# A graph-attention edge stage on one Trainium2 core: node ranges of 128 that start at multiples of 64, and gathers held to three groups ahead

## The chip, the cores and the metric

The kernel runs on one core of a Trainium2 chip. The metric is the device time of one execution in microseconds (us); the median of three runs of the kernel before is 867.32 us (866.72 to 867.4). Engines: PE is the matrix engine (TensorE), DVE is VectorE, ACT is ScalarE, POOL is GpSimd, SP is SyncE.

## The reference, cut to what matters

A graph attention layer over 2,500 nodes and 40,000 edges sorted by destination, then a mixture-of-experts layer. Only the first is touched:

```python
h = layernorm(x) @ W + b_w
s_dst, s_src = h @ a[:512], h @ a[512:]
e = leaky_relu(s_dst[dst] + s_src[src] + b_a, negative_slope=0.2)
w = jnp.exp(e)
alpha = w / segment_sum(w, dst)[dst]
x1 = x + segment_sum(alpha[:, None] * h[src], dst)
# then x1 + sum over the top 2 of 8 experts of share * (gelu(layernorm(x1) @ W1 + b1) @ W2 + b2)
```

## The kernel before, in words

**Three stages.** The node stage computes h for 20 tiles of 128 nodes and stores a table of rows of 516 floats in DRAM: h in two halves of 256, a one behind the first half (its sum is the denominator), and the two scores of the source. The edge stage sums weighted rows into `acc`, one slice of 2 x 257 floats for each tile of 128 nodes. The expert stage follows, once `acc` is divided and added to x.

**Edge stage.** The 40,000 edges are 313 chunks of 128, in 79 groups of four chunks (`GC`; the last group has one chunk). An average group of 512 sorted edges reaches over 2,500 / 79, some 32 nodes. Five engines work on a group g:

- POOL (`gather`, L501 to L509) issues one indirect DMA for each chunk, four a group, into slot g % 8 of the ring `rows` (`RING` is 8). It waits for the counter `agg_ok`, that is, until PE has done the sums of group g - 7. Its code is written out for all 79 groups.
- ACT (`weights`, L945) waits until all four chunks of the group are there (`got`), and for DVE's maximum of group g - 1 (the one PSUM buffer `ps_E2` is used again). It makes exp(s_dst + s_src) and exp(0.2 (s_dst + s_src)) for every edge of a chunk and all 128 nodes of the group's tile: eight instructions of 128 x 128.
- DVE (`step_of_group`, L1275) waits for ACT, computes the edge's lane in the tile (`lanes`, L1220), the larger of the two weights (`largest`, L1215), and four masks (`masked`, L1225), which keep a weight only where the node is the edge's own. Behind the masks of group g it adds the sums of group g - 2 to `acc` (`add_group`, L1290, and `add`, L1233), after a wait for `agg_ok`.
- PE (`group` and `sums`, L709 and L701) waits for the masks of group g and for `added` of group g - 2 (two pairs of PSUM banks take turns), and multiplies: 4 chunks x 2 halves of 257 columns, each float32 product two records in the trace, so 16 records a group. Its last one counts up `agg_ok`.

**Tiles that a group leaves.** A group whose edges go over from one tile of 128 nodes to the next has an extra round (`extras`, L1262, L955, and the loop at L718): ACT makes eight more activations for the next tile, DVE adds the sums of the extra before, makes lane, maximum and masks again, and PE does 16 more records into a third pair of banks (`ps_agg[2]`). One extra is added at the very end (L1321). A table of words, made on DVE at L1198 to L1212, tells every engine a group's tile, its number of extras, and how many came before.

**Order of the work.** Each engine runs its own program in order. ACT and PE loop over eight groups, DVE over four. POOL starts once the table of nodes is in DRAM (L512 to L514). ACT starts its first group when `sdst_b`, the destination scores of all nodes on all partitions, is copied from PSUM (L940 to L943) and the words are there.

Of the kernel before, what the change touches and what calls it, by code (L numbers as in the profile page):

```python
# [20 lines left out]
def gnn_moe_kernel(nc, x, src, dst, gnn_W, gnn_b_w, gnn_a, gnn_b_a, Wg, bg, W1, b1, W2, b2, out):  # L21
# [9 lines left out]
    RING = 8  # L31
    U = 4
# [8 lines left out]
    ONE, S_SRC = HD, 2 * HALF - 1  # L41

# [15 lines left out]
    with ExitStack() as ctx:  # L58
# [38 lines left out]
        acc = sg("acc", [P, NT, 2, HALF], F32, first)  # L97
# [143 lines left out]
        ps_E2, ps_id = ps[6].rearrange("p (c n) -> p c n", c=GC), ps[7][:, 0:P]  # L241
# [34 lines left out]
        acc_ok, added, xadded = sem("acc_ok"), sem("added"), sem("xadded")  # L276
# [84 lines left out]
        def tile_in(word):  # L361
            return field(word, 0, 31, NT - 1)

        def extra_in(word):
            return field(word, 5, 31, NT - 1)

        def before_in(word):
            return field(word, 10, 4095, NG * NT)

        def tile_of(value):  # L370
            return nc.s_assert_within(value, 0, NT - 1, skip_runtime_bounds_check_because="a tile of the window")
# [116 lines left out]
        def _(pool):  # L488
# [9 lines left out]
            nc.gpsimd.iota(node_id[:, :], pattern=[[1, NTN]], base=0, channel_multiplier=0)  # L498
# [376 lines left out]
        def _(act):  # L875
# [69 lines left out]
            def weights(q, r, tile, n=GC):  # L945

                low = E2x[:, 0, :, :] if q == 2 else ps_E2
                for k, (e, scale) in enumerate(((E1[:, q, :, :], 1.0), (low, SLOPE))):
                    for c in range(n):
                        bias = rows[:, r, c, S_SRC + k:S_SRC + k + 1]  # L950
                        m = nc.scalar.activation(e[:, c, :], sdst_b[:, bass.ds(tile * P, P)], ACT.Exp,  # L951
                                                 bias=bias, scale=scale)
                return m

            def extras(r, chunks):  # L955
# [3 lines left out]
                with act.If(extra > 0):  # L959
                    tile, before = act.snap(tile_in(word)), act.snap(before_in(word))  # L960
                    with act.Fori(0, extra) as n:
                        act.wait_ge(xmax_ok, before + n + 1)
                        weights(2, r, tile_of(tile + n + 1), chunks).then_inc(xexp_ok, 1)

            def group(r, i, chunks=GC):
                tile = act.snap(tile_in(act.snap(regs[r])))
                act.wait_ge(max_ok[(r + 1) % 2], RING // 2 * i + (r + 1) // 2 + 1)
                act.wait_ge(got[r], 16 * GC * (i + 1) if chunks == GC else 16 * (GC * i + chunks))
                weights(r % 2, r, tile, chunks).then_inc(exp_ok, 1)
                extras(r, chunks)  # L970

            act.wait_ge(d_ok, len(ps_d))
# [118 lines left out]
        def _(dve):  # L1091
# [116 lines left out]
            nc.vector.scalar_tensor_tensor(out=win_w[:, 0, BACK:NG + BACK], in0=win_n[:, 0, :], scalar=32.0,  # L1208
                                           in1=win_i[:, 0, :], op0=ALU.mult, op1=ALU.add)
            link(nc.vector.tensor_copy(win_w[:, 1, BACK + 1:NG + BACK], win_n[:, 1, 0:NG - 1]))  # L1210
            nc.vector.scalar_tensor_tensor(out=window[:, :], in0=win_w[:, 1, :], scalar=1024.0, in1=win_w[:, 0, :],
# [8 lines left out]
            def lanes(w, g, tile):  # L1220

                return nc.vector.tensor_tensor(lane[:, w, :], dstT[:, bass.ds(GC * g, GC)],  # L1222
                                               node_id[:, bass.ds(tile * P, 1)].to_broadcast([P, GC]), ALU.subtract)
# [9 lines left out]
            def add(q, tile, count):  # L1233
                a = acc[:, bass.ds(tile, 1), :, :].rearrange("p t a d -> p (t a) d")
# [325 lines left out]
```

## Time and profile before

| | |
|---|---|
| median of 3 runs | 867.32 us |
| the profiled execution: span from first to last instruction | 861.7 us |
| PE busy in the span | 696.6 us (81%) |
| DVE, ACT, POOL busy | 457.2, 415.4, 457.3 us |
| mean granted clock of PE | 0.921 |
| first gather of the edge stage issued | 92.24 us |
| last gather issued | 549.00 us |
| last addition to `acc` starts | 573.35 us |

The profile gives the span; of the time around it, it shows nothing, and the median lies 5.6 us above the span. Busy time counts matmuls as they are issued; their ends are modelled. A releaser "issue" means that the engine waited for nothing that the profile shows, "remote" that it was released by a semaphore whose sender is not told. In the rows below, `mean ns of one` is the duration of one instruction, and times of a timeline are counted from the start of the span.

### The profile page before, as it was taken

The page shows a single profiled execution, that of the slowest core. Times are in us where ns is not written, and L with a number is a line of the kernel's source. Part 1 is how long each engine was busy: PE and PEld are TensorE (multiplying, and loading weights), DVE is VectorE, ACT ScalarE, POOL GpSimd, SP SyncE. Part 2 cuts the span into 40 slices and gives each one's busy share as a digit, 9 for nine tenths or more (in the row PEclk, how much of TensorE's full clock was granted, in tenths as well). Part 3 has the DMA queues.
Part 4 walks back from the last instruction along what each step waited for, and adds up shares of the span by engine and source line. Part 5 has one row for each costly group of instructions (what it writes and reads, how often), then busy time and mean ns, then how long its engine had stood idle before and what let it go on. Part 6 is the DMA issues. An engine that isn't in the chain of part 4 may idle for free.

```text
span 861.7 us, 14833 instructions
## 1 busy us (share of the span) xinstructions
PE 696.6 (81%) x3260; PEld 553.6 (64%) x3261; DVE 457.2 (53%) x1232; ACT 415.4 (48%) x1134; POOL 457.3 (53%) x530
## 2 busy tenths in 40 slices
PE   4999355879888787879788888959889999999960
PEld 3777245657766666667676767845547787888840
DVE  5998223555555555556465555668485433333320
ACT  4443442545545554536455545618754444545430
POOL 5000575666666666666666666310105677777750
PEclk9999687998989899989999898988988999999995
DMA  5342576666666666666656666407993577777768
GB/s 197 117 155 92 156 213 164 172 188 168 186 181 174 178 177 182 186 171 183 189 166 184 176 179 179 118 27 283 334 380 127 104 131 131 135 131 135 130 91 250
DMA packets 58299, 146.96 MB, mean 171 GB/s; under 512 B 8868, under 2 KB 18708, under 8 KB 57880
## 3 DMA queue, kind: packets, MB, share of 16 engines
q0 software_dynamic: 35216, 106.84, 50.6%
q1 hardware_dynamic: 22968, 37.16, 12.3%
q10 hardware_dynamic: 80, 2.56, 1.0%
q8 instruction: 14, 0.23, 0.1%
q14 instruction: 21, 0.17, 0.1%
HBM read 118.17 MB, written 33.47 MB: 176 GB/s over the span
## 4 chain that ended last, share of the span: by engine, by line
PE 40%; issue 19%; DVE 11%; DMA 11%; ACT 4%; POOL 4%; POOLq 2%; DVEq 2%; another core or an unknown queue 2%; ACTq 1%; SPq 1%
PE ps L705 30%; DMA result<-y,si 8%; PE ps L659 3%; POOL rows L506 2%; DMA x_all<-in_x_dram 2%; ACT E L951 2%; ACT ps L951 2%; PE ps L844 1%; DVE Wt L1217 1%; PE ps L785 1%; DVE S L1228 1%; DVE acc L1235 1%; PE ps L755 1%; POOL xg L593 1%
## 5 line engine op out<-in xcount | busy, mean ns | idle before, releaser
L705 PE MATMUL ps<-rows,S 128*128 128x257 f32 x1556 | 383.4, 404 | 98.7 <-issue 83.9
L506 POOL DMA_INDIRECT rows<-node_table,srcT x313 | 301.8, 964 | 234.4 <-issue 83.8
L705 PEld LDWEIGHTS ps<-rows,S 128*128 128x128 f32 x1556 | 312.3, 202 | 169.6 <-issue 121.3
L951 ACT ACTIVATE E<-sdst_b,rows 128x128 f32 x389 | 124.0, 389 | 236.2 <-DVE Wt L1217 120.7
L1235 DVE TENSOR_TENSOR acc<-acc,ps 128x514 f32 x99 | 68.0, 687 | 116.1 <-remote 77.6
L1228 DVE SCALAR_TENSOR_TENSOR S<-ps,lane,Wt 128x128 f32<-128x128 f32 x389 | 109.6, 345 | 4.4 <-issue 0.8
L951 ACT ACTIVATE ps<-sdst_b,rows 128x128 f32 x313 | 96.2, 351 | 2.0 <-issue 2.0
L844 PE MATMUL ps<-W_e,xgT 128*128 x352 | 83.4, 380 | 0.0
L602 POOL DMA_INDIRECT result<-y,si x44 | 70.4, 1601 | 11.4 <-issue 7.1
L1222 DVE TENSOR_TENSOR lane<-dstT,node_id 128x4 f32 (+1 forms) x98 | 16.1, 164 | 111.5 <-issue 77.0
L844 PEld LDWEIGHTS ps<-W_e,xgT 128*128 128x128 f32 x352 | 63.4, 190 | 6.9
L659 PE MATMUL ps<-Wb,xT 128*128 128x512 f32 x240 | 59.1, 403 | 2.5 <-DVE dstT L1184 1.4
L858 PE MATMUL ps<-W_hi,hidT 128*128 x176 | 55.6, 437 | 3.0 <-DVE hidT L1512 2.8
L1058 ACT ACTIVATE act_h<-hid 128x256 f32<-128x256 f32 x44 | 18.4, 418 | 77.2 <-DVE hid L1519 67.2
L1529 DVE TENSOR_TENSOR y_b<-ps,b_b 128x512 f32<-128x512 f32 x44 | 30.4, 692 | 46.4 <-PE ps L858 39.4
L659 PEld LDWEIGHTS ps<-Wb,xT 128*128 128x128 f32 x240 | 45.6, 194 | 12.6 <-DVE dstT L1184 1.6
L1217 DVE SCALAR_TENSOR_TENSOR Wt<-E,ps 128x512 f32<-128x512 f32 (+1 forms) x79 | 53.3, 675 | 0.0
L593 POOL DMA_INDIRECT xg<-xn_table,gi x44 | 48.1, 1094 | 8.1 <-issue 4.6
L1519 DVE TENSOR_TENSOR hid<-ps,b_b 128x256 f32<-128x256 f32 x44 | 18.7, 424 | 55.1 <-PE ps L844 51.3
L551 POOL COPY si<-dst_row 128x1 int32 (+1 forms) x45 | 31.9, 709 | 19.0 <-DVE need L1503 11.9
L858 PEld LDWEIGHTS ps<-W_hi,hidT 128*128 128x128 f32 x176 | 32.6, 188 | 11.8 <-issue 5.9
L548 POOL COPY gi<-src_row 128x1 int32 (+1 forms) x45 | 9.7, 215 | 54.0 <-DVE src_row L1458 35.9
(203 smaller groups left out, 678.8 us busy)
## 6 DMA issues: line engine op xcount, KB each, us to landing
W_e<-in_L_ffn_W_dram SPq DMA_DIRECT2D x16, 512.0 KB, 8.5
node_table<-rows SPq DMA_DIRECT2D x20, 258.0 KB, 2.7
result<-acc SPq DMA_DIRECT2D x20, 256.0 KB, 2.5
xn_table<-xn SPq DMA_DIRECT2D x20, 256.0 KB, 2.2
rows<-node_table,srcT POOLq DMA_INDIRECT x313
x_all<-in_x_dram SPq DMA_DIRECT2D x19, 256.0 KB, 3.1
out_dram<-result SPq DMA_DIRECT2D x1, 2500.0 KB, 16.7
out_dram<-result ACTq DMA_DIRECT2D x1, 2500.0 KB, 18.4
```

The lines of the kernel that those rows point to most:

```text
L506: nc.gpsimd.indirect_dma_start(out=rows[:, g % RING, c, :], out_offset=None, in_=table, in_offset=bass.IndirectOffsetOnAxis(ap=srcT[:, GC ...
L551: nc.gpsimd.tensor_copy(si[:, r, :], dst_row[:, bass.ds(i, 1)]).then_inc(si_ok, 1)
L593: nc.gpsimd.indirect_dma_start(out=xg[:, r, :], out_offset=None, in_=xn_table, in_offset=bass.IndirectOffsetOnAxis(ap=gi[:, r, :], axis=0) ...
L602: nc.gpsimd.indirect_dma_start(out=result, out_offset=bass.IndirectOffsetOnAxis(ap=si[:, (r - LAG) % YR, :], axis=0), in_=y[:, (r - LAG) % ...
L659: m = pe.matmul(ps_h[s][j][:, :], xT[:, s, a, k, j * P:(j + 1) * P], Wb[:, b, k, :], start=(n == 0), stop=(n == 3 * KT - 1))
L705: m = pe.matmul(ps_agg[q][:, a, 0:HALF], S[:, w, c, :], rows[:, r, c, a * HALF:(a + 1) * HALF], start=(c == 0), stop=(c == n - 1))
L844: m = pe.matmul(ps_hid[1 - s][:, 0:F], xgT[:, 1 - s, k * P:(k + 1) * P], W1_e[:, bass.ds(e, 1), k, :].rearrange("p e f -> p (e f)"), start ...
L858: m = pe.matmul(ps_y[s][:, :], hidT[:, s, a, k * P:(k + 1) * P], W[:, bass.ds(e, 1), k, :].rearrange("p e d -> p (e d)"), start=(c == 0), ...
L951: m = nc.scalar.activation(e[:, c, :], sdst_b[:, bass.ds(tile * P, P)], ACT.Exp, bias=bias, scale=scale)
L1217: return nc.vector.scalar_tensor_tensor(out=Wt[:, q, 0:n, :], in0=E1[:, q, 0:n, :], scalar=FINITE, in1=(E2x[:, 0, 0:n, :] if q == 2 else p ...
L1228: m = nc.vector.scalar_tensor_tensor(out=S[:, w, c, :], in0=ps_id[:, :], scalar=lane[:, w, c:c + 1], in1=Wt[:, q, c, :], op0=ALU.is_equal, ...
L1235: nc.vector.tensor_tensor(a, a, ps_agg[q][:, :, 0:HALF], ALU.add).then_inc(count, 1)
```

## The change

Ranges of nodes ("windows") are still 128 wide, but start at multiples of 64, so there are 40 of them (`NW`); an even one is a tile, an odd one is the upper half of one tile and the lower half of the next. A group takes the window that starts at or below its first node, and has an extra only if it reaches 64 nodes or more beyond that window's half. The destination scores `sdst_w` are kept once for each window: ACT copies the even ones from PSUM as before, two new DVE copies make the odd ones. Partition p of an odd window stands for node 64 + p modulo 128 of its pair of tiles, so that `acc` need not move: the masks compare with numbers from `ps_id` that are turned by 64 for an odd window, and `add` is two instructions of 64 partitions, each into its own tile. The gather of group g waits for the sums of group g - 3 in place of g - 7; the ring keeps its eight slots. The code for extras stays.

```diff
+    AHEAD = 3
+    HP = P // 2
+    NW = 2 * NT
...
-        acc = sg("acc", [P, NT, 2, HALF], F32, first)
+        acc = sg("acc", [P, NT + 1, 2, HALF], F32, first)
...
-        sdst_b = sg("sdst_b", [P, NTN], F32, first)
+        sdst_w = sg("sdst_w", [P, NW, P], F32, first)
-        node_id = sg("node_id", [P, NTN], I16, first)
+        ring_id = sg("ring_id", [P, 3 * HP], I16, first)
+        base = sg("base", [P, NW], I16, first)
...
             def gather(g):
 
-                if g >= RING - 1:
-                    pool.wait_ge(agg_ok, g - RING + 2)
+                if g >= AHEAD:
+                    pool.wait_ge(agg_ok, g - AHEAD + 1)
...
-                nc.scalar.activation(sdst_b[:, 4 * b * P:4 * b * P + n], ps_d[b][:, 0:n], ACT.Copy).then_inc(d_ok, 1)
+                nc.scalar.activation(sdst_w[:, 8 * b:8 * b + 2 * n // P:2, :],
+                                     ps_d[b][:, 0:n].rearrange("p (t n) -> p t n", n=P), ACT.Copy).then_inc(d_ok, 1)
...
-            act.wait_ge(d_ok, len(ps_d))
+            act.wait_ge(odd_ok, 2)
...
-            link(nc.vector.tensor_single_scalar(win_i[:, :, :], win_i[:, :, :], 7, ALU.arith_shift_right))
-            link(nc.vector.tensor_tensor(win_n[:, 0, :], win_i[:, 1, :], win_i[:, 0, :], ALU.subtract))
+            link(nc.vector.tensor_single_scalar(win_i[:, :, :], win_i[:, :, :], HP.bit_length() - 1, ALU.arith_shift_right))
+            link(nc.vector.tensor_single_scalar(win_i[:, 0, :], win_i[:, 0, :], NW - 2, ALU.min))
+            link(nc.vector.tensor_tensor(win_i[:, 1, :], win_i[:, 1, :], win_i[:, 0, :], ALU.subtract))
+            link(nc.vector.tensor_single_scalar(win_i[:, 1, :], win_i[:, 1, :], 1, ALU.arith_shift_right))
+            link(nc.vector.tensor_copy(win_n[:, 0, :], win_i[:, 1, :]))
...
-            def masked(q, w, n=GC):
-
+            def masked(q, k, w, n=GC):
+
+                turn_of = dve.snap((w & 1) * HP)
                 for c in range(n):
                     m = nc.vector.scalar_tensor_tensor(
-                        out=S[:, w, c, :], in0=ps_id[:, :], scalar=lane[:, w, c:c + 1],
+                        out=S[:, k, c, :], in0=ps_id[:, bass.ds(turn_of, P)], scalar=lane[:, k, c:c + 1],
                         in1=Wt[:, q, c, :], op0=ALU.is_equal, op1=ALU.mult)
                 return m
 
-            def add(q, tile, count):
-                a = acc[:, bass.ds(tile, 1), :, :].rearrange("p t a d -> p (t a) d")
-                nc.vector.tensor_tensor(a, a, ps_agg[q][:, :, 0:HALF], ALU.add).then_inc(count, 1)
+            def add(q, w, count):
+
+                for part, tile in ((slice(HP, P), w >> 1), (slice(0, HP), (w + 1) >> 1)):
+                    a = acc[part, bass.ds(tile, 1), :, :].rearrange("p t a d -> p (t a) d")
+                    m = nc.vector.tensor_tensor(a, a, ps_agg[q][part, :, 0:HALF], ALU.add)
+                m.then_inc(count, 1)
...
             dve.wait_ge(d_ok, len(ps_d))
+            dve.wait_ge(ids_ok, 1)
+            nc.vector.tensor_copy(sdst_w[:, 1:NW:2, HP:P], sdst_w[:, 0:NW:2, HP:P]).then_inc(odd_ok, 1)
+            nc.vector.tensor_copy(sdst_w[:, 1:NW - 1:2, 0:HP], sdst_w[:, 2:NW:2, 0:HP]).then_inc(odd_ok, 1)
...
-            den = acc[:, :, 0, ONE]
+            den = acc[:, 0:NT, 0, ONE]
```

Left out of the diff: the fields of the words become one bit wider, names change from `tile` to `w`, extras step by two windows, and POOL fills `ring_id`, `base` and a corner of `sdst_w` in the node stage.

## Rows read from the trace of the kernel before

**Rows 1.** Busy time by stretch: start:end and length, then each engine's busy us (count), clock, DMA share, GB/s

```profile
92.00:166.00 74.00, 40.88 (x155) 33.34 (x156) 24.95 (x72) 26.89 (x90) 49.53 (x52) 0.77 0.67 186
308.00:355.00 47.00, 38.28 (x163) 31.16 (x162) 25.70 (x73) 25.69 (x86) 31.05 (x32) 0.96 0.65 177
544.00:575.00 31.00, 26.53 (x122) 22.51 (x120) 19.87 (x57) 12.56 (x42) 4.72 (x5) 1.00 0.17 48
```

**Rows 2.** Costliest groups of the page: busy us, mean ns of one, idle before

```profile
L705 PE MATMUL ps<-rows,S 128*128 128x257 f32 x1556 | 383.4, 404 | 98.7 <-issue 83.9
L506 POOL DMA_INDIRECT rows<-node_table,srcT x313 | 301.8, 964 | 234.4 <-issue 83.8
...
L1235 DVE TENSOR_TENSOR acc<-acc,ps 128x514 f32 x99 | 68.0, 687 | 116.1 <-remote 77.6
```

**Rows 3.** Timeline, first groups: start, duration, engine, line, count, idle before

```profile
92.24 1.15 POOL L506 DMA_INDIRECT rows<-node_table,srcT  x1 [78.54 <-DMA node_table<-rows]
...
96.22 0.95 POOL L506 DMA_INDIRECT rows<-node_table,srcT  x1 [0.30 <-issue]
...
100.09 1.28 ACT L951 ACTIVATE E<-sdst_b,rows 128x128 f32 x4 [8.20 <-DMA rows<-node_table,srcT]
101.21 0.95 POOL L506 DMA_INDIRECT rows<-node_table,srcT  x1 [0.30 <-issue]
...
102.73 0.16 DVE L1222 TENSOR_TENSOR lane<-dstT,node_id 128x4 f32<-128x4 f32 x1 [11.48 <-ACT ps L951]
...
103.53 1.13 DVE L1228 SCALAR_TENSOR_TENSOR S<-ps,lane,Wt 128x128 f32<-128x128 f32 x4
...
104.71 8.80 PE L705 MATMUL ps<-rows,S 128*128 128x257 f32 x32 [15.06 <-issue]
...
105.15 1.28 ACT L951 ACTIVATE E<-sdst_b,rows 128x128 f32 x4 [2.65 <-DMA rows<-node_table,srcT]
```

**Rows 4.** Timeline, who was released by the first two groups' sums

```profile
119.33 0.69 DVE L1235 TENSOR_TENSOR acc<-acc,ps 128x514 f32 x1 [4.64 <-remote]
...
137.08 0.95 POOL L506 DMA_INDIRECT rows<-node_table,srcT  x1 [4.91 <-remote]
```

**Rows 5.** Timeline of POOL: two gathers that waited, one group apart

```profile
195.88 0.94 POOL L506 DMA_INDIRECT rows<-node_table,srcT  x1 [2.41 <-remote]
201.89 0.94 POOL L506 DMA_INDIRECT rows<-node_table,srcT  x1 [1.32 <-PE ps L705]
```

**Rows 6.** Timeline, a stretch in which PE and DVE step slowly

```profile
288.39 0.38 PE L705 MATMUL ps<-rows,S 128*128 128x257 f32 x1 [2.43 <-issue]
...
289.82 0.16 DVE L1222 TENSOR_TENSOR lane<-dstT,node_id 128x4 f32 x1 [6.88 <-issue]
```

**Rows 7.** Timeline, the release of one group's sums late in the stage

```profile
319.96 0.94 POOL L506 DMA_INDIRECT rows<-node_table,srcT  x1 [2.19 <-remote]
319.97 0.69 DVE L1235 TENSOR_TENSOR acc<-acc,ps 128x514 f32 x1 [4.41 <-remote]
320.81 4.37 PE L705 MATMUL ps<-rows,S 128*128 128x257 f32 x19 [0.76 <-DVE acc L1235]
```

**Rows 8.** Timeline, the end of the edge stage

```profile
546.31 25.43 PE L705 MATMUL ps<-rows,S 128*128 128x257 f32 x116 [1.20 <-issue]
...
549.00 0.95 POOL L506 DMA_INDIRECT rows<-node_table,srcT  x1 [0.30 <-issue]
...
572.06 0.69 DVE L1235 TENSOR_TENSOR acc<-acc,ps 128x514 f32 x1 [0.21 <-DVE acc L1235]
573.35 0.69 DVE L1235 TENSOR_TENSOR acc<-acc,ps 128x514 f32 x1 [0.60 <-DVE acc L1235]
```

**Rows 9.** Busy time by stretch, columns as in the first group: the clock in the first groups

```profile
108.10:118.10 10.00, 5.41 (x25) 4.31 (x24) 3.44 (x11) 5.16 (x18) 7.56 (x9) 1.00 0.76 212
...
125.10:128.30 3.20, 1.17 (x6) 0.68 (x4) 0.00 (x0) 1.82 (x6) 2.59 (x3) 1.00 0.76 210
128.50:142.00 13.50, 4.07 (x10) 3.27 (x11) 3.60 (x11) 0.74 (x2) 6.77 (x7) 0.50 0.50 138
```

More of the change, by code:

```diff
@@ L358, in field, with window_in, window_of @@
                                       skip_runtime_bounds_check_because="the table's words are built so")
-        def tile_in(word):
-            return field(word, 0, 31, NT - 1)
+        def window_in(word):
+            return field(word, 0, 63, NW - 1)
         def extra_in(word):
-            return field(word, 5, 31, NT - 1)
+            return field(word, 6, 31, NT - 1)
         def before_in(word):
-            return field(word, 10, 4095, NG * NT)
-        def tile_of(value):
-            return nc.s_assert_within(value, 0, NT - 1, skip_runtime_bounds_check_because="a tile of the window")
+            return field(word, 11, 4095, NG * NT)
+        def window_of(value):
+            return nc.s_assert_within(value, 0, NW - 1, skip_runtime_bounds_check_because="a window of the nodes")
         block = ctx.enter_context(nc.Block())
@@ L942, in _, with weights @@
                 n = min(4, NT - 4 * b) * P
-                nc.scalar.activation(sdst_b[:, 4 * b * P:4 * b * P + n], ps_d[b][:, 0:n], ACT.Copy).then_inc(d_ok, 1)
-            def weights(q, r, tile, n=GC):
+                nc.scalar.activation(sdst_w[:, 8 * b:8 * b + 2 * n // P:2, :],
+                                     ps_d[b][:, 0:n].rearrange("p (t n) -> p t n", n=P), ACT.Copy).then_inc(d_ok, 1)
+            def weights(q, r, w, n=GC):
                 low = E2x[:, 0, :, :] if q == 2 else ps_E2
@@ L950, in weights @@
                         bias = rows[:, r, c, S_SRC + k:S_SRC + k + 1]
-                        m = nc.scalar.activation(e[:, c, :], sdst_b[:, bass.ds(tile * P, P)], ACT.Exp,
+                        m = nc.scalar.activation(e[:, c, :], sdst_w[:, bass.ds(w, 1), :].rearrange("p w n -> p (w n)"), ACT.Exp,
                                                  bias=bias, scale=scale)
@@ L1240, in settle, with weigh_extra, add_extra @@
                 nc.vector.memset(spare[:, 0:1], 0.0)
-            def weigh_extra(g, tile, at, chunks):
+            def weigh_extra(g, w, at, chunks):
                 dve.wait_ge(xS_ok, at)
                 dve.wait_ge(xexp_ok, at)
-                lanes(SR, g, tile)
+                lanes(SR, g, w)
                 largest(2, chunks).then_inc(xmax_ok, 1)
                 dve.wait_ge(xmax_ok, at + 1)
-                masked(2, SR, chunks).then_inc(xS_ok, 1)
-            def add_extra(n_added, tile, at):
+                masked(2, SR, w, chunks).then_inc(xS_ok, 1)
+            def add_extra(n_added, w, at):
                 if n_added is not None:
@@ L1254, in add_extra @@
                 dve.wait_ge(xagg_ok, at + 1)
-                add(2, tile, xadded)
+                add(2, w, xadded)
                 settle(xadded, at + 1)
-            last_tile = dve.alloc_register("last_extra_tile")
-            dve.reg_mov(last_tile, 0)
+            last_window = dve.alloc_register("last_extra_window")
+            dve.reg_mov(last_window, 0)
             def extras(g, n_added, word, chunks):
@@ L1265, in extras @@
                 with dve.If(extra > 0):
-                    tile, before = dve.snap(tile_in(word)), dve.snap(before_in(word))
-                    add_extra(n_added, tile_of(dve.snap(last_tile)), before)
-                    weigh_extra(g, tile_of(tile + 1), before + 1, chunks)
+                    w, before = dve.snap(window_in(word)), dve.snap(before_in(word))
+                    add_extra(n_added, window_of(dve.snap(last_window)), before)
+                    weigh_extra(g, window_of(w + 2), before + 1, chunks)
                     with dve.If(extra > 1):
                         with dve.Fori(1, extra) as n:
-                            add_extra(n_added, tile_of(tile + n), before + n)
-                            weigh_extra(g, tile_of(tile + n + 1), before + n + 1, chunks)
-                    dve.reg_mov(last_tile, tile + extra)
+                            add_extra(n_added, window_of(w + n + n), before + n)
+                            weigh_extra(g, window_of(w + n + n + 2), before + n + 1, chunks)
+                    dve.reg_mov(last_window, w + extra + extra)
             def step_of_group(g, r, i, first=False, chunks=GC):
@@ L1280, in step_of_group @@
                     dve.wait_ge(S_ok, g - 1)
-                tile = dve.snap(tile_in(word))
-                lanes(r % SR, g, tile)
+                w = dve.snap(window_in(word))
+                lanes(r % SR, g, w)
                 largest(r % 2, chunks).then_inc(max_ok[r % 2], 1)
                 dve.wait_ge(max_ok[r % 2], U // 2 * i + r // 2 + 2)
-                masked(r % 2, r % SR, chunks).then_inc(S_ok, 1)
+                masked(r % 2, r % SR, w, chunks).then_inc(S_ok, 1)
                 if not (first and r < 2):
@@ L1303, in _ @@
             dve.wait_ge(ids_ok, 1)
-            nc.vector.tensor_copy(ps_id[:, :], node_id[:, 0:P]).then_inc(id_ok, 1)
+            nc.vector.tensor_copy(ps_id[:, :], ring_id[:, :]).then_inc(id_ok, 1)
             dve.wait_ge(id_ok, 1)
```

33 lines of the change are left out of this document (18 added, 15 removed).

## The prediction

> **What bounds the kernel now.** I read the table of stretches first, then the costliest groups, then timelines of single groups.
>
> The edge stage runs from the first gather at 92.24 us to the last addition, which ends at 573.35 + 0.69 = 574.04 us: 482 of 861.7 us of span. The change touches nothing behind it. A stretch of eight groups takes about 47 us, and no engine fills it: PE 38.3, POOL 31.1, DVE and ACT 25.7 us [rows 1]. PE does 1,556 records: 79 groups are 78 x 16 + 4 = 1,252, and 19 extras of 16 are the other 304 [rows 2]. DVE's 99 additions tell the same: 79 + 19 + one at the end. PE's rate undisturbed is 25.43 / 116 = 0.219 us a record [rows 8], 3.5 us for 16.
>
> POOL is busy 0.96 us for a gather but starts one only every 1.25 us: 101.21 - 96.22 = 4.99 us for four [rows 3]. So 313 gathers need at least 391 us, 5.0 us a group. They take 549.00 - 92.24 = 456.8 us, 5.86 us a group. The difference is waiting for `agg_ok`. Then 25 us pass from the last gather to the last addition, with PE busy nearly throughout [rows 1, 8]: PE lies up to seven groups behind.
>
> **Two oddities matter.** First, what follows PE's sums is released late. PE issued groups 0 and 1 by 104.71 + 8.80 = 113.5 us [rows 3]; the addition of group 0 starts at 119.33, and the gather that needs group 1, that of group 8, at 137.08 [rows 4]. Again at 319.96 and 319.97 POOL and DVE are released together, after POOL had issued nothing for over 2 us [rows 7]. Where POOL issues just one group between two waits, the step is 201.89 - 195.88 = 6.01 us [rows 5], of which 4.7 are issues. Second, while gathers stream, PE and DVE sometimes crawl: gaps of 2.4 us before one matmul and 6.9 us before one lane instruction, with nothing to wait for [rows 6].
>
> **The change part by part.** The sum is made against the profiled execution, whose span stands 5.6 us below the median of 867.32; I carry the difference in time over to the median.
>
> Extras. A group of 512 edges reaches over some 32 nodes, a window from a multiple of 64 leaves at least 64, so I expect none. PE loses 304 records, 304 x 0.219 = 67 us, and DVE loses 19 additions, lanes, maxima and masks, ACT 19 x 8 activations. It is no term of the sum: whatever bounds the stage next takes its place. It would be POOL, at 5.0 us a group, if gathers could run ahead.
>
> The gather's wait. It closes a loop over three groups: gathers of g, their landing, ACT, DVE, PE, gathers of g + 3. Step by step:
> - four issues, first start to last end: 3 x 1.25 + 0.95 = 4.70 us [rows 3];
> - landing and ACT's start: 100.09 - (96.22 + 0.95) = 2.92, and 105.15 - (101.21 + 0.95) = 2.99: I take 2.95 [rows 3];
> - ACT's eight activations and the step to DVE: 102.73 - 100.09 = 2.64 [rows 3];
> - lane, maximum, masks: 103.53 + 1.13 - 102.73 = 1.93 [rows 3];
> - the additions of group g - 2, for which PE's sums of group g wait, stand behind these masks. One takes 0.687 us [rows 2]. Two halves of 64 partitions: between 0.69 us (if half the partitions took half the time) and 2 x 0.69. No row shows an instruction on 64 partitions. I take the upper end, since its 514 elements in a partition are as before; less the 0.1 us by which an addition starts before the masks end: 1.27;
> - DVE's addition to PE: 320.81 - (319.97 + 0.69) = 0.15 [rows 7];
> - 16 records of sums: 3.50 [rows 8];
> - release: 572.06 - (546.31 + 25.43) = 0.32, the nearest undisturbed one [rows 8].
>
> Together 17.46 us for three groups, 5.82 a group. That is over POOL's 5.0, so POOL waits every time. PE needs 3.5, DVE about 0.16 + 0.68 + 1.1 + 1.4 = 3.3 and ACT 2.5 us of it, so none becomes the bound, and the second addition costs time only as a link of the loop. The register steps for the turned numbers and for the second tile go beside running instructions, except some 0.1 us that may stand before the masks; as the bound I take three of the shortest DVE instructions seen, 3 x 0.16 us [rows 3], up to 0.5 us a loop, or 13 us in all.
>
> End of the stage. Group 78 follows group 0 by 26 loops: its gather starts at 92.24 + 26 x 17.46 = 546.2 us. It has one chunk, so group 77 is later: gathers from 102.46 (group 2's start, one step after 97.47) + 25 x 17.46 = 539.0, sums issued until 539.0 + 17.14 = 556.1, plus 0.9 for group 78: 557.0. Then the additions of groups 77 and 78 and of the last extra: before, they end 574.04 - 571.74 = 2.3 us behind PE; three more instructions of 0.69 make 4.4. End: 561.4, or 12.6 us earlier. The gain is the vanished backlog of PE, not the pace of the gathers, which hardly changes (5.82 against 5.86).
>
> Preparation. The two DVE copies of the odd windows (1,280 and 1,216 elements a partition) and three short steps for the words stand before ACT's first group. By 514 elements in 0.69 us [rows 2] they take 1.7 us each. ACT waits 8.2 us and DVE 11.5 us for the first rows at that time [rows 3], which hides them. If that cover were gone it would cost 4 us. A POOL that could not issue beside them would lose up to 3.4 us; I take 0.6. The Trainium skill ("SBUF — State Buffer", on the "DVE blocks DMA" trap) says that such a copy locks GpSimd out of descriptor writing while it runs. By it the first gather moves by up to the length of both copies; no row here shows such a pair.
>
> Sum: -12.6 + 0.6 = -12.0, that is 855 us.
>
> **The rivals.**
>
> *The release stays late, no change.* If PE's signal only gets through when the stream of gathers pauses, POOL's step is 6.01 us as in [rows 5], not 5.82. Then group 78 starts at 102.5 + 76 x 6.01 = 559.2; the end lies about 15.2 us behind (as 561.4 - 546.2), 574.4: 867 to 868 us. For it: [rows 4, 7]. Against: those signals came while PE had a backlog, here it has none.
>
> *PE falls to the low clock, slower.* PE will work 3.5 of 5.8 us and rest 2.3. In the first groups it was like that: the clock stayed at 1.00 (2.4 GHz) with PE busy 5.4 of 10 us, but went to 0.50 (1.2 GHz) after a stretch with 1.17 of 3.2 us [rows 9]. At 1.2 GHz sums take 3.5 us more, and the loop 21.0. It decides the sign once one loop in seven is hit: 26 x 3.5 / 7 = 13 us. One in three gives 855 + 26 x 3.5 / 3 = 885 us, every one 946. For it: the falls in [rows 9] follow scarce work. Against: 0.77 in the first stretch came with much longer rests. The Trainium skill ("TensorE: Matmul & The Clock Gate", "The HAM clock gate") calls the throttled state the default, which activity releases. By that rule a less busy PE loses clock, and the time is that of this rival.
>
> *POOL is the bound.* If the loop closes within 15 us, it is 5.0 us a group: 92.2 + 391 + 15 = 498, 76 us less, 791 us. It needs 2.5 us less than the rows give, such as landing in a quieter DMA (2.95 us is all of that link) or additions out of the way. Half of it (halves of additions at half time, landing 1 us shorter) gives a loop of 15.8: 43 us less than the forecast, 812 us.
>
> *The change doesn't do what it says*, and extras remain: then more than the loop's 17.46 us, by about 3.5 us an extra. A group of 64 nodes or more would be needed.
>
> **How the numbers follow.** 855 with chance 0.42; late release (862 to 872) 0.2; low clock (over 869) 0.28; a shorter loop (under 840) 0.09; extras 0.01. The range takes in both ends of the additions (26 x 0.69 = 18 us less) and of the register steps (13 us more), and low clock up to one loop in three: 835 to 885. The likeliest case's own range is 845 to 863. A measurement of this kernel can tell 0.2%, 1.7 us, from no change. Faster: 0.42 + 0.09 and 0.03 of the late release, 0.54; within 0.2%: 0.1; slower: 0.36.
>
> **What would show it.** 1,252 records of L705 and no E2x activations; 313 gathers, of which every fourth waits about 0.8 us, and steps of 5.8 us; 160 additions (two for each group and for the last extra) of 0.69 us; the last addition some 15 us behind the last gather; crawls as in [rows 6] gone. A step of 5.0 would show that I mis-sized the loop, 6.0 the late release, a clock below 0.9 in the stage the second rival.

## The result, and the profile after

The changed kernel takes 920.84 us (median of four runs, 911.06 to 933.7) where the kernel before takes 867.36 (866.72 to 867.48): a ratio of 1.057, interval 1.054 to 1.060. The slowest of the four, 933.7, lies over 1.5% above the fastest and is left out of the ratio. The forecast was 855 with a range of 835 to 885, so sign and range were both wrong. The profiled execution has a span of 909.4 us (861.7 before) and a mean granted clock of 0.882 (0.921 before).

The costliest groups of the page, columns as in [rows 2]:

```profile
L712 PE MATMUL ps<-rows,S 128*128 128x257 f32 x1252 | 348.8, 443 | 178.8 <-DVE acc L1249 149.2
L513 POOL DMA_INDIRECT rows<-node_table,srcT x313 | 296.2, 946 | 300.0 <-PE ps L712 111.3
...
L1249 DVE TENSOR_TENSOR acc<-acc,ps 64x514 f32 x160 | 110.1, 688 | 6.3 <-PE ps L712 1.9
```

There are 1,252 records and 160 additions, so no extras are left. The 304 fewer records, 67 us at the undisturbed rate, lower PE's busy time by only 383.4 - 348.8 = 34.6 us: the remaining ones are slower, 443 ns in place of 404. An addition of 64 partitions takes 0.688 us, the same as one of 128.

Busy time by stretch, columns as in [rows 1]:

```profile
92.00:166.00 74.00, 42.87 (x144) 34.08 (x144) 32.35 (x84) 26.55 (x86) 41.98 (x44) 0.77 0.57 160
...
214.00:261.00 47.00, 32.91 (x123) 26.42 (x122) 23.11 (x58) 17.96 (x60) 25.29 (x27) 0.83 0.54 149
261.00:308.00 47.00, 31.38 (x108) 24.82 (x107) 22.59 (x55) 15.61 (x52) 27.54 (x31) 0.82 0.59 165
308.00:355.00 47.00, 32.09 (x122) 25.23 (x121) 24.84 (x63) 18.11 (x61) 26.52 (x29) 0.89 0.56 159
...
575.00:626.00 51.00, 32.22 (x121) 25.55 (x119) 27.52 (x66) 15.12 (x50) 20.85 (x32) 0.86 0.39 110
```

PE has 32 of 47 us to do and runs at a clock of 0.82 to 0.89; before it had 38 us and 0.96. Some 29 gathers fall into 47 us where there were 32.

The timeline at the start and at the end of the edge stage:

```profile
93.15 0.83 DVE L1317 COPY sdst_w<-sdst_w 128x1280 f32<-128x1280 f32 x1
...
93.89 0.82 DVE L1318 COPY sdst_w<-sdst_w 128x1216 f32<-128x1216 f32 x1
94.33 1.34 POOL L513 DMA_INDIRECT rows<-node_table,srcT  x1 [81.89 <-DMA node_table<-rows]
...
102.36 1.28 ACT L959 ACTIVATE E<-sdst_w,rows 128x128 f32 x4 [7.42 <-DMA rows<-node_table,srcT]
...
607.72 0.94 POOL L513 DMA_INDIRECT rows<-node_table,srcT  x1 [2.00 <-PE ps L712]
...
622.64 1.39 DVE L1249 TENSOR_TENSOR acc<-acc,ps 64x514 f32 x2 [0.65 <-DVE acc L1249]
```

The stage runs from 94.33 to 622.64 + 1.39 = 624.03 us. It ends 50 us later than before (574.04), and 909.4 - 624.0 = 285.4 us lie behind it (287.7 before). So the loss is all in this stage. Its last gather starts 26 loops after its first: (607.72 - 94.33) / 26 = 19.75 us a loop of three groups, where the prediction has 17.46.

One such loop, from the first gather of a group to the first gather of the third group after it. The other groups' rows are left out:

```profile
258.82 0.94 POOL L513 DMA_INDIRECT rows<-node_table,srcT  x1 [3.89 <-PE ps L712]
...
262.57 0.95 POOL L513 DMA_INDIRECT rows<-node_table,srcT  x1 [0.30 <-issue]
...
264.33 3.74 PE L712 MATMUL ps<-rows,S 128*128 128x257 f32 x16 [2.31 <-DVE acc L1249]
...
266.54 1.28 ACT L959 ACTIVATE E<-sdst_w,rows 128x128 f32 x4 [6.21 <-DMA rows<-node_table,srcT]
...
269.26 0.16 DVE L1233 TENSOR_TENSOR lane<-dstT,base 128x4 f32 x1 [4.99 <-ACT ps L959]
269.34 0.68 DVE L1228 SCALAR_TENSOR_TENSOR Wt<-E,ps 128x512 f32<-128x512 f32 x1
270.25 1.12 DVE L1240 SCALAR_TENSOR_TENSOR S<-ps,lane,Wt 128x128 f32<-128x128 f32 x4 [0.23 <-issue]
...
271.41 1.39 DVE L1249 TENSOR_TENSOR acc<-acc,ps 64x514 f32 x2
...
272.95 9.51 PE L712 MATMUL ps<-rows,S 128*128 128x257 f32 x32 [4.88 <-DVE acc L1249]
...
279.26 0.94 POOL L513 DMA_INDIRECT rows<-node_table,srcT  x1 [4.08 <-PE ps L712]
```

The whole is 279.26 - 258.82 = 20.44 us. Link by link: issues until 263.52, 4.70; landing until 266.54, 3.02; ACT until 269.26, 2.72; lane, maximum and masks until 271.37, 2.11; additions until 272.80, 1.43; PE starts 0.15 later; then 6.31 us until POOL goes on. That last link is the odd one: 3.50 + 0.32 was forecast. The clock during it, columns as above:

```profile
264.20:268.20 4.00, 3.74 (x16) 2.95 (x16) 0.07 (x1) 1.66 (x6) 3.09 (x4) 1.00 0.77 215
268.20:272.90 4.70, 0.00 (x0) 0.00 (x0) 3.26 (x8) 1.96 (x8) 2.19 (x3) 0.78 0.51 140
272.90:278.70 5.80, 5.75 (x16) 4.72 (x17) 3.27 (x8) 1.67 (x7) 1.89 (x2) 0.59 0.54 155
278.70:282.50 3.80, 3.76 (x18) 2.94 (x16) 1.32 (x5) 1.94 (x7) 2.58 (x3) 1.00 0.33 83
```

PE works at 1.00 (2.4 GHz), rests for 4.9 us, and while it rests the mean clock falls to 0.78. The 16 records after the rest take 5.75 us at 0.59, that is some four fifths of this time at the lower level (0.5, 1.2 GHz). The next 18 are at 1.00 again. This recurs: of the 78 full sets of sums, 32 take over 4.2 us from their first to their last start, 5.0 us in the median where undisturbed ones take 3.3, and in most of the stage it is every third set. All 14 sets that began over 4 us after the start of PE's record before were slow, and none of the 32 that began within 2 us; of the 31 between, 17 were.

### The profile page after: what moved, and what is told of

Its sections match the earlier page's. It is cut to its first block, busy times and chain, and to the rows that moved or that the text cites. A ratio compares the mean times of both kernels' runs of the same rounds, so it can differ in the third digit from the quotient of the medians.

```text
span 909.4 us, 13772 instructions
## 1 busy us (share of the span) xinstructions
PE 660.4 (73%) x2956; PEld 517.4 (57%) x2957; DVE 467.9 (51%) x1165; ACT 370.4 (41%) x982; POOL 450.5 (50%) x533
## 4 chain that ended last, share of the span: by engine, by line
PE 31%; issue 18%; POOL 13%; DVE 13%; DMA 10%; ACT 5%; DVEq 3%; another core or an unknown queue 2%; POOLq 1%; ACTq 0%; SPq 0%
POOL rows L513 12%; PE ps L712 11%; DMA rows<-node_table,srcT 6%; PE ps L851 5%; PE ps L865 4%; PE ps L666 3%; ACT ps L959 2%; DVE acc L1249 2%; DMA result<-y,si 2%; PE ps L762 2%; ACT E L959 2%; DVE Wt L1228 2%; PE ps L841 1%; DVE S L1240 1%
## 5 line engine op out<-in xcount | busy, mean ns | idle before, releaser
L712 PE MATMUL ps<-rows,S 128*128 128x257 f32 x1252 | 348.8, 443 | 178.8 <-DVE acc L1249 149.2
L513 POOL DMA_INDIRECT rows<-node_table,srcT x313 | 296.2, 946 | 300.0 <-PE ps L712 111.3
L712 PEld LDWEIGHTS ps<-rows,S 128*128 128x128 f32 x1252 | 276.7, 226 | 250.7 <-issue 184.0
L959 ACT ACTIVATE E<-sdst_w,rows 128x128 f32 x313 | 100.0, 390 | 329.3 <-DMA rows<-node_table,srcT 322.1
L1233 DVE TENSOR_TENSOR lane<-dstT,base 128x4 f32 (+1 forms) x79 | 13.2, 167 | 245.4 <-ACT ps L959 158.0
L1249 DVE TENSOR_TENSOR acc<-acc,ps 64x514 f32 x160 | 110.1, 688 | 6.3 <-PE ps L712 1.9
L1240 DVE SCALAR_TENSOR_TENSOR S<-ps,lane,Wt 128x128 f32<-128x128 f32 x313 | 88.2, 345 | 18.7 <-issue 11.1
L959 ACT ACTIVATE ps<-sdst_w,rows 128x128 f32 x313 | 95.9, 350 | 0.0
## 6 DMA issues: line engine op xcount, KB each, us to landing
out_dram<-result ACTq DMA_DIRECT2D x1, 2500.0 KB, 18.1
```

The costliest lines, as they stand in the source:

```text
L513: nc.gpsimd.indirect_dma_start(out=rows[:, g % RING, c, :], out_offset=None, in_=table, in_offset=bass.IndirectOffsetOnAxis(ap=srcT[:, GC ...
L712: m = pe.matmul(ps_agg[q][:, a, 0:HALF], S[:, w, c, :], rows[:, r, c, a * HALF:(a + 1) * HALF], start=(c == 0), stop=(c == n - 1))
L959: m = nc.scalar.activation(e[:, c, :], sdst_w[:, bass.ds(w, 1), :].rearrange("p w n -> p (w n)"), ACT.Exp, bias=bias, scale=scale)
L1240: m = nc.vector.scalar_tensor_tensor(out=S[:, k, c, :], in0=ps_id[:, bass.ds(turn_of, P)], scalar=lane[:, k, c:c + 1], in1=Wt[:, q, c, :], ...
L1249: m = nc.vector.tensor_tensor(a, a, ps_agg[q][part, :, 0:HALF], ALU.add)
```

## The experiments

Each ratio is against the kernel before in the same job, on the same chip. The chips differ: the kernel before took 787.9 us (786.1 to 789.9) in the first job and 868.8, 869.9 and 863.8 in the three others. The first job's chip is called the fast chip here.

**Fill TensorE's rest.** Ten products of the identity with itself go into an unused corner of PSUM after each set of sums, for groups 0 to 71:

```diff
                 sums(r % 2, r % SR, r, chunks).then_inc(agg_ok, 1)
+                if not (isinstance(g, int) and g >= RING):
+                    for _ in range(10):
+                        pe.matmul(ps[5][:, 384:512], ident[:, :], ident[:, :], start=True, stop=True)
```

> The changed kernel, with ten float32 products of 128 x 128 that nobody reads behind the sums of each of groups 0 to 71, in a bank of PSUM that the sums do not use. They fill PE's rest (about 0.107 us a record, 20 records, 2.1 us) and are nothing to the result. Clock theory (the loop of three groups costs 17.9 us at 2.4 GHz, and one set of sums at 1.2 GHz on the same chain of groups adds some 2.3 us each time round): the clock in the edge stage goes to 0.98 or more, no set of sums takes over 3.6 us from first to last issue, the loop falls from 20.2 to about 18 us, and the time to 867 to 878 us. Rival (the late release of PE's signal while gathers stream is what costs, and more records on PE make it later): clock up, but steps between gathers stay at 6.6 us and the time stays over 905 us.

Measured on the fast chip: 876.76 us (873.78 to 880.74), ratio 1.115, interval 1.111 to 1.119; first to last gather 479.9 us, 18.46 us a loop. Time and loop are as expected; two of the 78 full sets are still slow.

> The changed kernel (gathers three ahead) with ten small products a group that fill PE's rest, as in the first run with warm filling, on whichever chip this job gets (the kernel before took 788 us on one and 869 us on another). Theory A: the loop of three groups is latency bound and its half-clock set of sums is the larger part of the loss; then this kernel does not depend on the chip, 870 to 882 us, with every set of sums at 3.3 us, and on a chip where the kernel before takes 868 it is 1 to 2% slower than it, so five sixths of the changed kernel's loss is clock. Theory B: late release of the gathers adds to it on the chips where before shows it: over 890 us there, with late waits in the trace. Theory C: the products themselves cost more than they save on such a chip: as slow as the changed kernel, 911 to 930.

> The changed kernel itself, unchanged, beside the other runs of this job. Theory A: its loop of three groups is latency and clock bound, with no term that differs between chips, so it is 911 to 930 us on any chip, also where before takes 788 (a ratio of 1.17 there, 1.06 to 1.07 on the others). Theory B: late release makes part of its loss on the slower chips: then on a chip where before takes 788 it is 10 to 30 us shorter, 885 to 905 us, with no late wait.

On a slower chip the filled kernel takes 878.68 us (876.29 to 883.51), ratio 1.0095, interval 1.007 to 1.012, and the changed kernel beside it 914.08 us (905.4 to 921.17), ratio 1.054, interval 1.048 to 1.060 (1.06 to 1.07 was expected). One stretch of the two, the filled one first:

```profile
261.00:308.00 47.00, 44.17 (x278) 40.13 (x277) 24.73 (x60) 18.26 (x61) 28.96 (x31) 1.00 0.61 169
```

```profile
261.00:308.00 47.00, 32.51 (x122) 25.51 (x120) 23.79 (x60) 16.87 (x56) 26.74 (x29) 0.87 0.57 158
```

More work for PE, 12 us in 47, makes the kernel 914.1 - 878.7 = 35.4 us faster: only 3 sets of sums are slow in place of 31. The filled kernel takes the same on both chips within 2 us, though the kernel before differs by 82 us between them. So of the changed kernel's loss of 914.1 - 869.9 = 44 us, 35 us or four fifths went with the slow sets (five sixths were expected). The late releases of the gathers went too: 18 in the changed kernel's profile of this job, 28 us in sum, against 24 short ones, 12 us. What each was worth is worked out behind the experiments. That the changed kernel itself does not depend on the chip is not shown, for it did not come onto the fast one.

**Each half of the change alone.** The windows without the wait (lead back at seven groups), and the wait without the windows:

```diff
-    AHEAD = 3
+    AHEAD = 7
```

> The changed kernel with AHEAD = 7, so that a gather waits for the sums of the group seven back, as before. Loop theory (the wait of three groups is what made it slower): the loop then allows 17.9 / 7 = 2.6 us a group, POOL's 5.0 us or the release of PE's signals bounds; between 795 us (POOL alone, 5.0 us a group) and 860 us. Rival (windows of 64, with two additions a group and the turned masks, cost what was lost): no faster than 900 us.

```diff
-                if g >= RING - 1:
-                    pool.wait_ge(agg_ok, g - RING + 2)
+                if g >= 3:
+                    pool.wait_ge(agg_ok, g - 2)
```

> The kernel before with one line changed: the gather waits for the sums of the group three back. Loop theory: the loop is one addition and the register steps shorter (16.9 us at the high clock), but every fourth group has an extra of 16 records and a second round on ACT and DVE in it (about 4 us more each), so 6.3 us or more a group, 900 to 950 us. Rival (the windows are the cause): within 2% of 867 us.

On the fast chip the windows alone take 790.28 us (788.03 to 794.34), ratio 1.004, interval 1.002 to 1.005, 5 us under the range that was expected; the wait alone 885.15 us (884.09 to 889.51), ratio 1.125, interval 1.122 to 1.129. A stretch of the windows alone, and then the stage's gathers in that kernel:

```profile
261.00:308.00 47.00, 35.38 (x153) 27.93 (x152) 31.05 (x78) 21.94 (x73) 35.43 (x39) 1.00 0.75 212
```

```profile
L513 POOL DMA_INDIRECT rows<-node_table,srcT x313 | 296.4, 947 | 177.3 <-issue 95.1 <-DMA node_table<-rows 82.2
```

POOL waits for nothing in the stage but its own issuing: 38 gathers in 47 us, 5.0 us a group (485.16 - 94.64 = 390.5 us for all). That is the rival "POOL is the bound", whose 791 us came true for the lead of seven, on this chip. There the wait is what costs, with or without the windows. The wait alone came out below the 900 us and more that was expected: with its extras PE is busy 36 of 47 us and rests less, and the clock is 0.90 where the changed kernel, on another chip, has 0.82 to 0.89. That this is the reason is not tested:

```profile
261.00:308.00 47.00, 36.26 (x145) 29.52 (x145) 22.07 (x64) 21.61 (x72) 28.47 (x31) 0.90 0.64 178
```

**One addition for two.** All 128 partitions are added to one tile, so the halves of odd windows go to the wrong nodes:

```diff
-                for part, tile in ((slice(HP, P), w >> 1), (slice(0, HP), (w + 1) >> 1)):
+                for part, tile in ((slice(0, P), w >> 1),):
```

> The changed kernel with one addition of 128 partitions a group, into the lower tile alone (sums of odd windows go to wrong rows for half the nodes, which no wait depends on). Loop theory: the second addition is a link of the loop; 0.69 us less for three groups, 26 x 0.7 = 18 us less than the changed kernel's 911 to 934 us, if the clock falls as often. Rival (additions lie beside other work): no more than 3 us less.

One run took 901.5 us; first to last gather is 512.1 us, 19.70 us a loop, no better than the 19.69 to 20.16 of the changed kernel's three profiles. In 253 cases the next record of a set starts 0.40 to 0.50 us later, the pace of the low clock (256 in the profile above). Taking 0.69 us out of a link gave no visible gain in the loop, against the 18 us expected, and the trace shows where it went: from a group's first gather to its sums the way is 13.30 us in place of 14.06, but the 26 sets on the chain that sets the pace are all slow and take 6.0 us in the median, where the changed kernel's slow sets take 5.0. They begin 6.4 us after the start of PE's record before, in the median (3.8 in the changed kernel). No gather was released late in this run, so the slow sets alone make a loop of 19.70 us. On the run's total nothing is concluded: it is a single run on another chip.

**The lead between three and seven, on slower chips.** Beside them a profile of the kernel before and one of the changed kernel:

> The kernel before, unchanged, for its profile on the chip of the experiments. Late-release theory (what held the kernel before at 867 us was PE's signals coming through only when the gathers paused, and that differs from chip to chip): where the kernel before takes 788 us, its profile shows no wait of POOL for agg_ok, gathers every 5.0 us a group, and no stretch in which PE and DVE step every 0.7 us; where it takes 867 us, the waits and the slow stretches are there again. Rival (the matmuls or the DMA themselves are faster there): records closer than 0.217 us, or landings well under 2.9 us.

> The changed kernel, unchanged, beside the others of this job. Loop theory: it waits in every group, for a loop that holds no signal held back by the stream if the chip has none; so 900 to 925 us on any chip, and against a kernel before of 788 us a ratio of 1.14 to 1.17. Rival (the chip matters as much as for the kernel before): 80 us less than 920, about 840 us.

> The changed kernel with AHEAD = 7 once more. On a chip where the kernel before takes 788 us: 788 to 794 us again. On a chip where it takes 867 us: the release theory says that POOL now streams with six groups of room, so PE's signals wait for a pause that comes late: 820 to 880 us, with stretches of slow steps on PE and DVE longer than before; POOL-bound theory says 800 us or less there too.

> The changed kernel with AHEAD = 5. Loop theory: 17.9 us over five groups is 3.6 us a group, and even 20.3 us is 4.1, both under POOL's 5.0: no wait is left where no signal is late, and the time is that of AHEAD = 7 within 3 us. Rival (any wait nearer than the ring costs): between AHEAD 7 and 3, 20 us or more over AHEAD 7.

> The changed kernel with the lead of the gathers four groups in place of three. Theory A: a lead of three loses because its loop (18.0 us undisturbed, 20.3 with a half-clock set) must pass for every three groups. With four groups in the loop it gives 20.3/4 = 5.1 us a group, so the loop is no longer what holds the gathers; on this chip, where a stream of gathers without a pause lets TensorE's signals through late, the late releases come back and the time is that of a lead of five, 852 to 866 us. Theory B: the half-clock sets come with any wait for the sums and lengthen the loop further: a lead of four lies between, 875 to 900 us. Where before takes 788, theory A gives 786 to 800.

| lead | us (range) | ratio, interval | starts at the low clock's pace | us a group |
|---|---|---|---|---|
| before, 7 | 868.82 (867.32 to 871.84) | 1 | 125 of 1,556 records | 5.93 |
| 3 | 926.72 (911.04 to 930.02) | not used | 245 of 1,252 records | 6.72 |
| 4 | 851.76 (851.14 to 854.55) | 0.9875, 0.985 to 0.991 | 168 | 5.83 |
| 5 | 858.08 (857.75 to 859.42) | 0.988, 0.985 to 0.990 | 161 | 5.88 |
| 7 | 864.23 (863.31 to 866.07) | 0.995, 0.993 to 0.997 | 167 | 5.88 |

A start counts where the next record starts 0.40 to 0.50 us later, within a set; the pace is first to last gather by 78. The lead of four was in a later job, where the kernel before took 863.83. The changed kernel's own runs scatter most, so its row is not compared as a whole, and its ratio of 1.054 is taken from the job with the filled kernel. One group more in flight turns this into 0.9875: 44 us lost become 12 us gained, some 56 us. The leads of seven and four came as expected. The lead of five was to equal the lead of seven within 3 us and was 6 us faster, and the changed kernel, expected at 900 to 925 us, was at 927. With four or more groups the loop no longer holds the gathers, as expected, and the late release of [rows 4] comes back: each of the 34 or 35 gathers that waited was released late. The timeline of POOL and PE with a lead of four:

```profile
250.77 0.94 POOL L513 DMA_INDIRECT rows<-node_table,srcT  x1 [1.91 <-PE ps L712]
...
253.20 8.87 PE L712 MATMUL ps<-rows,S 128*128 128x257 f32 x32 [3.96 <-DVE acc L1249]
...
259.54 0.95 POOL L513 DMA_INDIRECT rows<-node_table,srcT  x1 [0.30 <-issue]
262.40 0.95 POOL L513 DMA_INDIRECT rows<-node_table,srcT  x1 [1.91 <-PE ps L712]
```

Eight gathers (9.7 us) go out without a pause, POOL stops for 1.91 us, and everything passes at once: 11.63 us for two groups, 5.82 a group.

**What lets the signals through.** Three more kernels ask for the late release. One has five groups of lead and three PSUM pairs in turn, so that PE may be a group further:

```diff
-                    pe.wait_ge(added, g - 1)
-                sums(r % 2, r % SR, r, chunks).then_inc(agg_ok, 1)
+                    pe.wait_ge(added, g - 2)
+                sums(r % 3, r % SR, r % RING, chunks).then_inc(agg_ok, 1)
```

> Gathers five ahead and three PSUM pairs in turn instead of two, so TensorE may run one group further before the additions must have read a pair (the code for extra sets, which these inputs never use, is left out). Theory A: on a chip where before takes 868 the signals of TensorE pass in bursts when the gather stream drains, and a burst can carry as many groups as there are buffers; three groups a drain of about 15 + 1.9 us give 5.6 us a group and 840 to 850 us. Theory B: the bursts are limited by the gathers' lead or by something else: 855 to 865, as with five ahead and two pairs. On a chip where before takes 788 both give 786 to 794, GpSimd's 5.0 us a group being the bound.

This kernel also leaves out the code for extras and has PE's and DVE's loops written out longer, so its time is not that of the third pair alone. It takes 852.79 us (850.82 to 853.98), ratio 0.980, interval 0.978 to 0.982: the best ratio of all. Its gathers go out twelve at a time:

```profile
304.23 0.95 POOL L513 DMA_INDIRECT rows<-node_table,srcT  x1 [2.85 <-remote]
304.30 1.39 DVE L1238 TENSOR_TENSOR acc<-acc,ps 64x514 f32 x2 [5.01 <-remote]
...
318.02 0.95 POOL L513 DMA_INDIRECT rows<-node_table,srcT  x1 [0.30 <-issue]
...
321.85 0.95 POOL L513 DMA_INDIRECT rows<-node_table,srcT  x1 [2.88 <-remote]
321.94 1.39 DVE L1238 TENSOR_TENSOR acc<-acc,ps 64x514 f32 x2 [4.96 <-remote]
```

Three groups a pause, as theory A says, but the pause grew from 1.9 to 2.9 us, and the pace is 17.62 / 3 = 5.87 us a group in place of 5.6: the gathers take 456.1 us in all where a lead of five with two pairs has 458.8. Another 2 us come from the end of the stage, 16.1 us behind the last gather in place of 18.1. The expected 840 to 850 was missed by 3 us.

The second fetches half of each row, the third fills TensorE's rest with a lead of four:

```diff
-                        out=rows[:, g % RING, c, :], out_offset=None, in_=table,
+                        out=rows[:, g % RING, c, 0:258], out_offset=None, in_=table.rearrange("n (a d) -> (n a) d", a=2),
```

> Gathers seven ahead, with as many gather instructions and descriptors, but each fetches half a row (258 values in place of 516); the sums take the same half twice, so the output is other than the reference's. Theory A: what delays TensorE's signals on the slower chip is the gathers' bytes in flight; half of them gives no late wait, 5.0 us a group, about 790 us. Theory B: it is GpSimd's issuing or the number of descriptors, whatever the bytes: late waits as with seven ahead, about 864 us on a chip where before takes 868. On a chip where before takes 788 both say 785 to 792, and nothing is told apart.

> A lead of four groups, and ten small products a group that fill TensorE's rest. Theory A: the undisturbed loop of 18.4 us holds four groups, 4.6 us a group, under GpSimd's 5.0, so nothing but late release can hold the gathers; the products take 19 us more of TensorE in a group's 5.0 to 5.9 us only if it is late, so the time is that of the lead of four without them or up to 10 us more, 850 to 870 us, with late waits in the trace. Theory B: warm products keep TensorE's signals from passing early or late alike and the loop stays the bound: 870 to 885 us as with a lead of three. Where before takes 788, theory A gives 790 to 805 and no wait at all.

Half rows: 865.34 us in one run, with 37 late releases as with full rows (35), and 92 GB/s in place of 182:

```profile
261.00:308.00 47.00, 32.17 (x128) 25.89 (x127) 27.32 (x69) 20.82 (x70) 30.75 (x34) 0.89 0.33 92
```

So the bytes are not what delays the signals, as far as one run can show it. The filled kernel with a lead of four takes 864.13 us (862.18 to 865.32), ratio 1.0005, interval 0.999 to 1.002, 12 us over the lead of four without the products where at most 10 were expected, with a wait before nearly each group:

```profile
242.69 0.94 POOL L513 DMA_INDIRECT rows<-node_table,srcT  x1 [1.33 <-remote]
...
244.96 2.39 PE L723 MATMUL ps<-ident 128*128 128x128 f32 x20
...
246.44 0.95 POOL L513 DMA_INDIRECT rows<-node_table,srcT  x1 [0.30 <-issue]
...
248.70 0.94 POOL L513 DMA_INDIRECT rows<-node_table,srcT  x1 [1.32 <-remote]
```

The gather at 248.70 waits for the sums that stand ahead of the products at 244.96, so PE had them issued 3.7 us before. POOL goes on 1.31 us after its own last issue has ended, as at 242.69. The step is 6.01 us, exactly that of [rows 5]. The clock is 1.00, columns as in [rows 1]:

```profile
200.00:300.00 100.00, 96.62 (x600) 87.77 (x600) 54.70 (x134) 39.95 (x133) 63.05 (x67) 1.00 0.63 175
```

PE is busy for 97 of 100 us here. From group 20 to group 59 its sums start 1.8 to 3.7 us after the addition that they wait for, so it is always somewhat behind. Within each eight groups this lag shrinks (from 3.7 to 2.1 us between groups 48 and 54), so PE alone would go faster than 6.01 us a group.

## Why the prediction was wrong

**The counts and most links were right.** No extras, 313 gathers, 160 additions of 0.69 us, and the last addition 624.03 - 607.72 = 16.3 us behind the last gather (15.2 forecast). That two halves cost twice one whole, the upper bound that was taken, was right. The removed work bought nothing, as written: on the two chips the windows alone change the time by +0.4 and -0.5%.

**The loop was forecast too short by its small links.** Undisturbed ones measure 4.70 for the issues, 2.95 to 2.99 landing, 2.72 ACT, 2.12 to the masks' end (a gap of 0.24 us stands before the masks, where the register step was priced at 0.1), 1.42 additions, 0.15, 3.33 from the sums' first to their last start, and 0.65 for the release (0.32 forecast from a row of DVE, not of POOL). That is 18.04 to 18.08 us against 17.46, some 16 us over 26 loops, over the 13 us that were kept as a bound for the register steps. With it alone the kernel would have been at about 870, no faster than before.

**The failed step is the term "16 records of sums: 3.50" in the loop, and behind it the rival on the clock, in its "one loop in seven", "one in three gives 885".** The term is the pace of [rows 8], where PE did not rest; on the chain that sets the pace the sums took over 5 us. The rival took a slow set of sums as an accident that meets some loops, with a chance of 0.28, because PE works 3.5 of 5.8 us. But the chain paces itself: one group in three comes after PE's longest rest, 4.9 us in the rows above, and its sums are slow. They end late and send POOL on late, and so the rest before the same chain's next sums is long again. The other two chains' groups are issued behind it in order and gain nothing from being earlier. So about one set of sums in three is slow, and each loop pays: 26 x (19.75 - 18.06) = 44 us. A slow set takes 4.9 to 6.3 us in place of 3.3, less than the 3.5 us more of the rival, because part of it is at the high clock; what was wrong is how often. The price of "every loop" stood in the text, 946 us at the full price. At 1.7 us a loop the sum closes: 867.3 - 12.6 + 16 + 44 is 914.7, plus 2.1 us for a later start and 1.1 for the longer end, less 2.3 that the work behind the stage took less, is 915.6, against a span of 909.4 + 5.6 = 915.0. The filled kernels show this term: without the slow sets 35 us come back, and the ten products themselves lengthen the loop by about 0.4 us (18.46 against 18.06), 10 us; together 45.

A late release could have been the cause in its place, for the filled products took away both. The chain settles it. Followed back from the last gather, each time to what it had waited for, the profile after has 22 passes of the loop (three groups each) and 12 steps of POOL alone (one group each). All 22 sets on it are slow and add 42 us; late releases add 14 us, of which the steps of POOL, 5.0 us where a group of the loop takes 6.0, give 12 back. With one addition, on the fast chip, the chain is 26 passes without a late release, and its slow sets add 63 us.

The Trainium skill ("TensorE: Matmul & The Clock Gate", "The HAM clock gate") calls the throttled state the default, which activity releases. The trace agrees: after a rest of 4.9 us the clock is 0.59. The prediction cited that rule and gave it the smaller chance, on the ground that 5.4 of 10 us busy had held 1.00 in [rows 9]. That row was no guide: in the stretches after PE is busy 31 to 33 of 47 us, a larger share than there, and the clock fell all the same, in the rests between.

**The late release was judged rightly in part.** It was said to belong to a PE with a backlog. Of 49 groups that waited in the profile after, 18 were still released over 0.35 us later than the usual 0.65, by 31 us in sum, where before all 37 were, by 211 us. And it does not need a backlog:

```profile
244.07 3.71 PE L712 MATMUL ps<-rows,S 128*128 128x257 f32 x16 [2.36 <-DVE acc L1249]
...
250.24 0.94 POOL L513 DMA_INDIRECT rows<-node_table,srcT  x1 [2.03 <-remote]
```

PE had rested before these sums, had all of them issued by 247.41, and the gather that waits for them starts 2.83 us later, after POOL had issued two groups without a pause. What the late ones have in common is that stream of gathers. With a lead of three the loop itself makes most of the pauses.

**Preparation.** The copies take 0.83 us each, half of the 1.7 estimated, and are hidden: ACT waits 7.42 us behind them. The first gather starts 2.1 us later than in the profile of before, but its releaser is the last store of the table, and a second profile of before has its first gather at 93.88, so the copies need not be the reason. The gather itself starts at 94.33 beside the second copy and takes 1.34 us, where it took 1.15 before. The Trainium skill ("SBUF — State Buffer", on the "DVE blocks DMA" trap) says that GpSimd cannot write a DMA's descriptors while such a copy runs. The trace neither shows nor excludes it: the gather outlasts the copy, which ends at 94.71, and at most the 0.2 us more would be its price.

## What to carry to other kernels

A wait that closes a loop over few groups must be priced by that loop's latency with every engine at its worst state in it, since an engine that is idle once a loop may be slow once a loop, and a slow link on the one chain that sets the pace is paid in full each time. A gain on another link of that chain can be lost again in the same way: with one addition PE rested longer in one piece and its sums became slower. Ask after each added wait how long TensorE then rests in one piece, not what share of the time it is busy. A lead one group longer, a change of one constant, was worth 56 us here, so a depth is worth a sweep before it is judged.

## What the runs showed of the hardware

**Chips differ.** The same kernel of before takes 788 us on one chip and 864 to 870 on the others. The lead of seven shows how: on the fast chip no gather waits and PE's clock is 1.00 (row above); on another its 35 waits are all released late, 205 us in sum. Whether the kernel before gains its 80 us in the same way was not profiled.

**The late release comes with an unbroken stream of gathers, and not from its bytes.** With one, two or three groups between pauses the step is 6.01, 11.63 and 17.62 us, 5.8 to 6.0 us a group, however the work around it is arranged. That the pace stays while the pauses change from 1.3 to 2.9 us is not explained: whether POOL's issuing, the number of descriptors or something else on these chips sets it stays open, as does why one chip is free of it.
